# VectorE's product of uyy with the square of ux ahead of the addition of K

## The reference

```
ux, uy, uxx, uxy, uyy = Sobel derivatives of u, each clipped to +-10
g2 = ux*ux + uy*uy
K = clip((uxx*uyy - uxy*uxy) / ((1 + g2)^2 + eps), -5, 5)
H = ((1 + uy*uy)*uxx - 2*ux*uy*uxy + (1 + ux*ux)*uyy) / (2*sqrt(1 + g2 + eps)^3 + eps)
u = u + 0.01 * clip(alpha*K + beta*clip(H, -5, 5), -1, 1)     # ten times, edges copied
x1 = 0.7*u + 0.3*x
out = conv3x3(relu(conv3x3(x1, w1, b1)), w2, b2) + x1         # 16 channels to 16
```

## Time and profile before

| | |
|---|---|
| median of three runs | 38,702.86 us |
| the profiled execution | 38,698.44 us |
| its span (first to last instruction) | 38,696.7 us |
| VectorE busy | 34,434.0 us (89%) |
| TensorE busy (matmuls) | 34,434.2 us (89%) |
| ScalarE busy | 33,167.9 us (86%) |
| GpSimd busy | 20,465.8 us (53%) |
| mean granted TensorE clock | 0.992 of full speed |

### The profile page before, as it was taken

How to read it: one execution, slowest core, us unless ns; L and a number is a source line. 1 busy time by engine, 2 the same in 40 slices (tenths; PEclk the granted TensorE clock), 3 DMA queues, 4 the chain that set the end, 5 groups by cost and what they waited for, 6 DMA issues and landing times. The chain is left out here.

```text
span 38696.7 us, 453600 instructions
## 1 busy us (share of the span) xinstructions
PE 34434.2 (89%) x126400; PEld 23294.9 (60%) x126400; DVE 34434.0 (89%) x33108; ACT 33167.9 (86%) x33722; POOL 20465.8 (53%) x7685
## 2 busy tenths in 40 slices
PE   5888888888888888888888888888888888889999
PEld 3666666666666666666666666666666666666666
DVE  8999999999999999999999999999999999993111
ACT  5999999999999999999999999999999999994333
POOL 3555555555555556555555555555555555550000
PEclk9999999999999999999999999999999999999999
DMA  5333333333333333333333333333333333333333
GB/s 189 83 83 82 82 75 78 83 83 82 82 83 83 82 79 74 81 83 83 83 82 83 83 83 76 77 81 83 83 83 82 83 83 80 73 82 83 87 87 85
DMA packets 2687511, 3261.71 MB, mean 84 GB/s; under 512 B 2266180, under 2 KB 2266308, under 8 KB 2364740
## 3 DMA queue, kind: packets, MB, share of 16 engines
q1 hardware_dynamic: 2686276, 3247.70, 33.5%
HBM read 582.33 MB, written 268.44 MB: 22 GB/s over the span
## 5 line engine op out<-in xcount | busy, mean ns | idle before, releaser
L646 PE MATMUL tame_slot<-tame_split,tame_M 128*128 128x512 f32 x51200 | 15156.1, 418 | 4131.5 <-DVE tame_ux L517 3386.6
L646 PEld LDWEIGHTS tame_slot<-tame_split,tame_M 128*128 128x128 f32 x51200 | 9160.8, 190 | 10140.8 <-issue 2690.5
L646 PE MATMUL tame_slot<-tame_halo,tame_M 128*128 128x512 f32 x51200 | 14319.2, 402 | 0.0
L356 POOL TENSOR_TENSOR tame_split<-tame_U,tame_split 128x1024 fp32r<-128x1024 f32 x2560 | 6232.0, 2434 | 12755.0 <-ACT tame_split L391 12755.0
L646 PEld LDWEIGHTS tame_slot<-tame_halo,tame_M 128*128 128x128 f32 x51200 | 9757.9, 191 | 2513.8
L368 POOL TENSOR_TENSOR tame_ux<-tame_ux,tame_cross 128x1024 f32<-128x1024 f32 x2560 | 8071.5, 3153 | 433.4 <-POOL tame_ux L362 433.4
L362 POOL TENSOR_TENSOR tame_ux<-tame_ux,tame_uy 128x1024 f32<-128x1024 f32 x2560 | 6161.8, 2407 | 972.6 <-DVE tame_uy L517 972.6
L431 ACT ACTIVATE tame_slope<-tame_slope 128x2048 f32<-128x2048 f32 x2560 | 4895.4, 1912 | 0.0
L656 PE MATMUL tame_slot<-tame_uxy,tame_unit 128*128 128x512 f32 x10240 | 4810.6, 592 | 5.4 <-DVE tame_slot L540 5.4
L426 ACT ACTIVATE tame_slope<-tame_slope 128x1024 f32<-128x1024 f32 x2560 | 2716.8, 1061 | 2141.4 <-issue 2139.4
L559 DVE TENSOR_TENSOR tame_uyy<-tame_slot,tame_slope 128x1024 f32<-128x1024 f32 x2560 | 3132.2, 1223 | 945.6 <-PE tame_slot L656 938.1
(11 more groups left out here) (74 smaller groups left out, 38207.5 us busy)
## 6 DMA issues: line engine op xcount, KB each, us to landing
tame_halo<-tame_split SPq DMA_DIRECT2D x2560, 520.0 KB
tame_halo<-tame_split SPq DMA_DIRECT2D x2560, 260.0 KB
tame_halo<-tame_split SPq DMA_DIRECT2D x5120, 65.0 KB
tame_U<-in_x SPq DMA_DIRECT2D x256, 512.0 KB, 3.9
tame_stage<-in_x SPq DMA_DIRECT2D x128, 1024.0 KB, 4.9
mixed<-tame_stage SPq DMA_DIRECT2D x128, 1024.0 KB, 6.4
out<-res SPq DMA_DIRECT2D x672, 192.0 KB
xin<-mixed SPq DMA_DIRECT2D x344, 256.0 KB, 4.6
```

Source lines behind the costliest of these rows:

```text
L356: nc.gpsimd.tensor_tensor(split_rows(c, 1), half_rows(c), split_rows(c, 0).bitcast(F32), ALU.subtract).then_inc(lo_ready, 2)
L646: last = nc.tensor.matmul(ps[name][:, b * BANK:(b + 1) * BANK], M[0:lanes, matrix, :], rows(c, part)[:, b * y:(b + 1) * y, :], start=(n < ...
```

## The change

`add_k` of half k-1 and `term_uyy` of half k change places in VectorE's list. `clip` of uyy goes with the product, but does nothing in the tame variant. All waits and signals stay with their instructions.

```diff
--- before.py
+++ after.py
@@ -622,10 +622,12 @@
                     curvature_h(t, k - 1)
                     clip_k(t, k - 1)
                     clip_h(t, k - 1)
-                    add_k(t, k - 1)
                 if exists(kind, k):
                     clip("uyy", t, k)
                     term_uyy(t, k)
+                if exists(kind, k - 1):
+                    add_k(t, k - 1)
+                if exists(kind, k):
                     clip("uxy", t, k)
                     clip("uxx", t, k)
```

## The result

The kernel after takes 46,062.74 us in the median of four runs (46,056.25 to 46,092.25), beside 38,698.72 us for the kernel before in the same comparison: 19% slower, ratio 1.1904, 95% interval 1.1884 to 1.1925. The forecast was 46,000 us.

The account below looks back on a forecast made before the run. Bound by a 13.32 us loop of VectorE's row and TensorE's chain from cross term to K product. 38,698 plus 4,454 holding plus 3,070 clock falls less 230 hidden gives 45,990, said as 46,000 us; range 42,600 to 47,500.

Parts of the forecast that it names:

- The wait ahead of ux is not on the loop: TensorE's 1.29 us wait for the uyy product does not set the period; ending it gains at most 0.03 us.
- K's addition and GpSimd's low part meet: After the swap, VectorE's addition of K starts 0.23 us after GpSimd's low part has started.
- Rival (b): VectorE's addition of K gets in first and the low part is held: 39,930 us; chance 0.10.
- A hold for a whole instruction: VectorE's addition of K ends 1.09 us after GpSimd's low part, adding 1.74 us a period.
- rival (c): VectorE and GpSimd take turns instead of holding: at most 2,790 us more, so 41,490 us; chance 0.05.
- An idle of 3.05 us ahead of uy: TensorE runs no matmul for 3.05 us between ux's end and uy, against 1.29 us idle before.
- falls of the clock in four of five periods: TensorE's clock drops to its lower level, 1.2 GHz, behind the longer idle in 0.8 of the periods, an estimate.
- The price of a fall and its cover: Each TensorE clock fall costs 1.5 us; in 256 blend periods VectorE's blend hides some 0.9 us, -230 us.
- The sum: Whole kernel: 38,698 + 4,454 + 3,070 - 230 = 45,990 us, said as 46,000 us.
- The holding: Delay of VectorE's addition of K by GpSimd's low part, over 2560 periods: 4,454 us.
- The clock's term: TensorE's slower clock behind the idle ahead of uy: 3,070 us, less 230 us hidden by blends.

Follow-up runs that it names:

- after_short_low: Kernel after, with GpSimd's low part computed for only 64 of 1024 columns: 38,702.55 us, ratio 1.0001.
- before_short_low: Kernel before, with GpSimd's low part computed for only 64 of 1024 columns: 38,702.03 us, ratio 1.0000.
- after_low_in_two: Kernel after, with the low part in two GpSimd instructions of half the size, same work: 41,212.95 us, ratio 1.0651.
- after_ux_twice: Kernel after, with TensorE computing the ux derivative twice in a row, same result: 43,167.91 us, ratio 1.1155.
- one_pass_copy_first: Kernel before, with squared uxy and its subtracting matrix as fp32r, and ScalarE copying uyy ahead of the slope's square: 38,691.73 us, ratio 0.9997.
- k_behind_uxx: Kernel after, with K's addition moved behind the next period's uxx product: 41,046.75 us, ratio 1.0608.
- after_low_waits: Kernel after, with GpSimd's low part waiting for K's addition of the same period: 40,949.06 us, ratio 1.0581.

## Why the prediction was right

- **The wait ahead of ux is not on the loop, so the earlier uyy product gains nothing.** Right: after_short_low and before_short_low differ by 0.5 us in 38,702.
- **K's addition and GpSimd's low part meet, 0.23 us apart.** Right: 0.24 us, and in 2,552 of the 2,560 periods the addition ends 1.08 us behind the low part (counted over the trace; near the other eight additions there is no low part). Rival (b) is out.
- **A hold for a whole instruction, to 1.09 us after GpSimd's end, +1.74 us a period.** Right: 1.08 us after, and 15.06 us in the period shown, 15.08 in the mean of those with a full clock and no blend. after_low_in_two shows that it is the instruction that is held for, which the three rows of before had only implied; rival (c) is out.
- **An idle of 3.05 us ahead of uy, and falls of the clock in four of five periods.** Right in the idle, 3.01 and 3.07 us. The share came out at 78%, and that was luck: the rows of before showed only that 2.0 us was sometimes enough, and four in five was picked between none and all.
- **The price of a fall and its cover.** The lengths of the periods, from K product to K product over the whole trace after, give both. Without a blend, 1,808 periods with a stretch at half clock last 16.68 us in the mean and 497 at full clock 15.08: 1.61 us a fall where 1.5 was set, 2,904 us in all. With a blend, 200 with such a stretch last 16.99 and 54 without 16.71: 0.28 us a fall, 57 us in all. The clock's part is thus 2,961 us where the forecast had 2,840, and after_ux_twice gives back 2,895 of it. The cover behind the blends came near the 230 us that were set (200 x 1.33 = 266), by two errors that oppose each other: 0.9 us was taken off in all 256 periods, though falls were set in four of five only, which would be 184 us; and 1.33 us of a fall is hidden there, not 0.9.
- **The sum.** 45,990 against 46,062.74. The holding was met within some 50 us: 46,062.74 - 38,698.72 - 2,961 = 4,403 us by the count of falls, and 4,465 by after_ux_twice, against 4,454. The clock's term was about 120 us short, by the price of a fall. So the mechanism carries the number, and the lucky part is the share of falls: a tenth more or less of it would have moved the forecast by some 370 us (0.1 x 2,304 x 1.61).

Rival (b) was right in kind and wrong in price when it was made to happen: it left out the hop to GpSimd and ScalarE's chain behind the addition of H.

## What to carry to other kernels

Before two instructions of VectorE change places, ask of each whether it reads two SBUF tensors, and lay GpSimd's row beside both places: one step of 1.1 us moved the addition from 0.90 us ahead of a GpSimd instruction's start to 0.24 us behind it, and cost 1.74 us a period, more than the instruction itself. An engine made to wait on the path of TensorE may cost twice, once in the wait and again in the clock behind it; idle filled with repeated matmuls gave back 2.9 ms of 7.4. And a wait that is long is not for that a wait that counts: the 1.29 us ahead of ux were worth nothing, the 0.42 us ahead of the K product 0.4 ms.

## What the runs showed of the hardware

- Who goes first is settled within some tens of nanoseconds between the two recorded starts. In one_pass_copy_first, counted over the trace, the addition of K was held in all 208 periods in which it started between 11 ns ahead of the low part and 26 ns behind it, and ran free in all others, in which it started at least 15 ns ahead (six of them by 30 ns or less). In the kernel after, where it started 148 to 513 ns behind, it was held each time.
- The clock fell in 78% of idles of 3.0 us, in about a fifth of those of 1.8 to 2.0 us in k_behind_uxx (530 of 2,522), in all 208 of 3.8 to 4.6 us in one_pass_copy_first, and in none of those of 1.2 to 1.4 us in any run here. In the kernel before, 131 of 184 idles of about 2.0 us had a fall behind them, so the length of the idle alone does not give the share; what else does was not tried.
- A hop from VectorE's end to a GpSimd instruction that waits for it took 0.23 us in the rows shown and 0.22 us in the median (after_low_waits).
